# First expert layer: one float32 product split into three fp32r products of leading and trailing bits

## The reference

```python
aff = feats @ centroids.T                 # feats: the layer-normed tokens, 3200 x 256
eid = jnp.argmax(aff, axis=1)             # one expert for each token
xhat = (feats - mu) * jax.lax.rsqrt(var + EPS)
for e in range(E):                        # E = 8, w1[e]: 256 x 1024, w2[e]: 1024 x 256
    mask = (eid == e).astype(feats.dtype)[:, None]
    h = xhat * gamma[e] + beta[e]
    y = feats + jax.nn.relu(h @ w1[e] + b1[e]) @ w2[e] + b2[e]
    alpha = jax.nn.sigmoid(feats @ centroids[e])[:, None]
    out = out + mask * (alpha * y + (1.0 - alpha) * feats)
```

## Time and profile before

| | |
|---|---|
| median of 3 runs | 1718.27 us (1717.52 to 1718.36) |
| the profiled execution | 1719.54 us |
| its span in the profile | 1717.6 us |
| stage `experts` in it: first matmul of tile 0 | 1421.48 us from the start |
| stage `experts` in it: last scatter starts | 1711.74 us from the start |
| mean granted TensorE clock | 0.946 |

### The profile page before, as it was taken

The page is one execution under the profiler, slowest core; times in us unless marked ns, Lnnn a source line. Parts: engine busy times, 40 slices in busy tenths (PEclk is TensorE's granted clock), DMA queues, the critical chain, the costliest instruction groups (busy, mean ns, idle before and its releaser), DMA issues. The chain is left out here.

```text
span 1717.6 us, 39303 instructions
## 1 busy us (share of the span) xinstructions
PE 1512.1 (88%) x12244; PEld 1299.5 (76%) x12244; DVE 1057.3 (62%) x2627; ACT 763.3 (44%) x1830; POOL 426.4 (25%) x564
## 2 busy tenths in 40 slices
PE   4799999999999999829999999999996309999997
PEld 3687878787878787727888888888885307888886
DVE  5658585858585857426777777677773305555553
ACT  3536363646464646314555555655652002222221
POOL 4112121212121211142222222222212153333332
PEclk9999999999999999868999999999997558999999
DMA  5703030303030303057667667677651243555551
GB/s 181 194 1 78 1 76 0 76 0 76 0 76 0 76 0 77 1 131 202 179 184 199 184 183 197 181 192 191 180 135 51 53 134 116 180 184 178 180 179 50
DMA packets 159949, 195.71 MB, mean 114 GB/s; under 512 B 83724, under 2 KB 128307, under 8 KB 159636
## 3 DMA queue, kind: packets, MB, share of 16 engines
q1 hardware_dynamic: 154356, 186.09, 39.7%
q0 software_dynamic: 3968, 6.59, 1.2%
q10 hardware_dynamic: 1568, 2.30, 0.4%
HBM read 138.63 MB, written 58.05 MB: 115 GB/s over the span
## 5 line engine op out<-in xcount | busy, mean ns | idle before, releaser
L1198 DVE TENSOR_REDUCE row_max<-psb_s 100x1 f32<-100x361 f32 x512 | 263.5, 531 | 143.5 <-PE psb_s L1341 137.5
L1090 ACT ACTIVATE probs<-psb_t 121x400 f32<-121x400 f32 (+1 forms) x384 | 190.4, 507 | 114.2 <-PE psb_t L1351 111.7
L419 POOL TENSOR_TENSOR diag<-neg_ident,row_max 100x400 fp32r<-100x400 f32 x128 | 112.2, 898 | 375.1 <-PE ps_t L666 203.6
L1341 PE MATMUL psb_s<-k,q 97*100 97x362 f32 x512 | 186.2, 367 | 15.4 <-DVE row_max L1198 8.3
L1351 PE MATMUL psb_t<-q,k 98*121 98x200 f32 (+1 forms) x768 | 147.4, 274 | 2.6 <-ACT probs L1090 2.0
L2021 PE MATMUL psd_h<-h_in,w_sb 128*128 128x256 f32 x640 | 143.8, 383 | 1.4 <-ACT h_in L1887 1.4
L2029 PE MATMUL psd_y<-w_sb,hid 128*128 128x256 f32 x640 | 144.5, 379 | 0.0
L2021 PEld LDWEIGHTS psd_h<-h_in,w_sb 128*128 128x128 f32 x640 | 123.2, 193 | 19.0 <-issue 1.8
L2029 PEld LDWEIGHTS psd_y<-w_sb,hid 128*128 128x128 f32 x640 | 120.1, 190 | 15.5
L1351 PEld LDWEIGHTS psb_t<-q,k 98*121 98x121 f32 (+1 forms) x768 | 125.5, 184 | 7.6 <-ACT probs L1090 5.1
L376 ACT CAST o_hi<-ps_ot 64x200 fp32r<-64x200 f32 x256 | 82.1, 321 | 100.1 <-PE ps_ot L691 95.2
(11 more groups left out here) (225 smaller groups left out, 3674.7 us busy)
## 6 DMA issues: line engine op xcount, KB each, us to landing
w_sb<-in_w SPq DMA_DIRECT2D x40, 1024.0 KB, 7.8
packed_keys<-k_st SPq DMA_DIRECT2D x32, 724.0 KB, 3.7
k<-packed_keys SPq DMA_DIRECT2D x64, 362.0 KB
v_rows<-v_tok SPq DMA_DIRECT2D x32, 400.0 KB
v_ext<-v_rows SPq DMA_DIRECT2D x32, 400.0 KB
q<-packed_queries SPq DMA_DIRECT2D x64, 200.0 KB
k<-packed_keys SPq DMA_DIRECT2D x64, 181.0 KB
c_t<-in_contextT SPq DMA_DIRECT2D x32, 361.0 KB, 4.6
```

The costliest lines, as they stand in the source:

```text
L419: pool.tensor_tensor(diag[:, g % 2], c.neg_ident[0:S, 0:S].unsqueeze(1).to_broadcast([S, GH, S]), row_max[:, g // 2 % 2, g % 2].unsqueeze( ...
L1090: act.activation(probs[0:KT[kt], u % 2, kt], ps_t[i % 2][0:KT[kt], 0:4 * S], ACT.Exp, scale=HD2 ** -0.5).then_inc(probs_ready, 1)
L1198: dve.reduce_max(row_max[:, p, h:h + 1], ps_s[h % 2][0:S, 0:S2], AX_X).then_inc(max_ready, 1)
L1341: pe.matmul(ps_s[h % 2][0:S, 0:S2E], q2[0:97, p, u, g, S * a:S * (a + 1)], k2[0:97, p, u, g], start=True, stop=True).then_inc(scores_ready, 1)
```

## The change

Each tile's `h_in` and each tile's first-layer weights are split into leading bits (a cast to fp32r) and trailing bits (the difference), and the first layer becomes `split3`. `w1_hi` is made by ACT in two parts of 512 columns, `w1_lo` by POOL in four parts of 256 columns, `h_hi` by ACT and `h_lo` by DVE. The splits of w1 run ahead: at step j ACT makes `w1_hi` of tile j+2, POOL the second half of `w1_lo` of tile j+1 and the first half of that of tile j+2. The load of w1 gets a semaphore of its own and is issued one tile earlier than that of w2. PE waits for `h_lo`, and for `w1_lo` part by part. Some semaphores are made once for all stages.

```diff
@@ experts, SP
                     reach(sp, y_filled, NH * (j - 1))
-                    load_weights(sp, c, e, p, w1, w2)
+                    load_w2(sp, c, e, p, w2)
                 if not last:
                     load_rows(j + 1, 1 - p)
+                    if not (isinstance(j, int) and j < 1):
+                        e = expert_of(sp, c, j + 1)
+                        sp.wait_ge(w1_lo_ready, LO_PARTS * j)
+                        load_w1(sp, c, e, 1 - p, w1)
@@ experts, POOL
+            def trailing_bits(j, p, first, end):
+                for n in range(first, end):
+                    cols = slice(F // LO_PARTS * n, F // LO_PARTS * (n + 1))
+                    pool.wait_ge(w1_hi_ready, j * HI_PARTS + (n * HI_PARTS // LO_PARTS + 1))
+                    pool.sem_inc(pool_passed, 1)
+                    pool.tensor_tensor(w1_lo[:, p, :, cols], c.w1_sb[:, p, :, cols], w1_hi[:, p, :, cols].bitcast(F32),
+                                       ALU.subtract).then_inc(w1_lo_ready, 1)
             prepare(0, 0)
+            trailing_bits(0, 0, 0, LO_PARTS)
+            trailing_bits(1, 1, 0, LO_PARTS // 2)
             def step(j, p, last):
                 if not last:
                     prepare(j + 1, 1 - p)
+                    trailing_bits(j + 1, 1 - p, LO_PARTS // 2, LO_PARTS)
+                if not (isinstance(j, int) and j + 2 >= TILES):
+                    trailing_bits(j + 2, p, 0, LO_PARTS // 2)
                 finish(j, p)
@@ experts, ACT, prepare
                 ins.then_inc(h_in_ready, 1)
+                act.wait_ge(h_in_ready, j + 1)
+                act.sem_inc(act_passed, 1)
+                act.copy(h_hi[:, p], h_in[:, p]).then_inc(h_hi_ready, 1)
                 act.wait_ge(z_ready, j + 1)
                 act.activation(ez[:], z[:], ACT.Exp, scale=-1.0).then_inc(ez_ready, 1)
+            def leading_bits(j, p):
+                act.wait_ge(c.w1_loaded[p], (j - p) * 8 + 16)
+                reach(act, hid_filled, NF * (j - 1))
+                act.sem_inc(act_passed, 1)
+                for n in range(HI_PARTS):
+                    cols = slice(F // HI_PARTS * n, F // HI_PARTS * (n + 1))
+                    act.copy(w1_hi[:, p, :, cols], c.w1_sb[:, p, :, cols]).then_inc(w1_hi_ready, 1)
@@ experts, ACT, step
                 if not last:
                     prepare(j + 1, 1 - p)
+                if not (isinstance(j, int) and j + 2 >= TILES):
+                    leading_bits(j + 2, p)
@@ experts, DVE (behind weigh, ahead of y)
+            def low_inputs(j, p):
+                dve.wait_ge(h_hi_ready, j + 1)
+                dve.sem_inc(dve_passed, 1)
+                dve.tensor_tensor(h_lo[:, p], h_in[:, p], h_hi[:, p].bitcast(F32), ALU.subtract).then_inc(h_lo_ready, 1)
@@ experts, PE
-                pe.wait_ge(c.w_loaded[p], (j - p) * 16 + 32)
-                pe.wait_ge(h_in_ready, j + 1)
+                pe.wait_ge(h_lo_ready, j + 1)
                 for f in range(NF):
                     if f >= 4:
                         copied(j, f - 4)
+                    if f % (NF // LO_PARTS) == 0:
+                        pe.wait_ge(w1_lo_ready, j * LO_PARTS + (f * LO_PARTS // NF + 1))
                     for k in range(KD):
-                        ins = pe.matmul(ps_h[f % 4][:, 0:T], c.w1_sb[:, p, k, 128 * f:128 * (f + 1)], h_in[:, p, k],
-                                        start=(k == 0), stop=(k == KD - 1))
+                        cols = slice(128 * f, 128 * (f + 1))
+                        ins = split3(pe, ps_h[f % 4][:, 0:T], w1_hi[:, p, k, cols], w1_lo[:, p, k, cols],
+                                     h_hi[:, p, k], h_lo[:, p, k], k == 0, k == KD - 1)
                     ins.then_inc(hid_filled, 1)
                 reach(pe, y_ready, NH * j)
+                pe.wait_ge(c.w2_loaded[p], (j - p) * 8 + 16)
```

More of the change, by code:

```diff
@@ L162, in self_attention @@
         ps_y = [ps_p[0], ps_ot]
-        dve_passed = sem("dve_passed_a")
-        pool_passed = sem("pool_passed_a")
+        dve_passed = c.dve_passed
+        pool_passed = c.pool_passed
         x_first = sem("x_first")
@@ L776, in cross_attention @@
         ps_f = psum("psb_f", [128, 512])
-        act_passed = sem("act_passed")
-        dve_passed = sem("dve_passed")
-        pool_passed = sem("pool_passed")
+        act_passed = c.act_passed
+        dve_passed = c.dve_passed
+        pool_passed = c.pool_passed
         w_loaded = sem("w2_loaded")
@@ L1502, in expert_buffers @@
     c.tables = ctx.enter_context(nc.semaphore("tables4"))
-    c.w_loaded = [ctx.enter_context(nc.semaphore(f"w4_loaded{p}")) for p in range(2)]
+    c.w1_loaded = [ctx.enter_context(nc.semaphore(f"w41_loaded{p}")) for p in range(2)]
+    c.w2_loaded = [ctx.enter_context(nc.semaphore(f"w42_loaded{p}")) for p in range(2)]
 def expert_of(eng, c, j):
@@ L1508, in expert_of, with load_w1, load_w2 @@
                           else c.tile_expert[0:1, bass.ds(j, 1)], min_val=0, max_val=E - 1)
-def load_weights(sp, c, e, p, w1, w2):
+def load_w1(sp, c, e, p, w1):
     sp.dma_start(c.w1_sb[:, p], w1[bass.ds(e, 1)].rearrange("o (k p) n -> p (o k) n", p=128)
-                 ).then_inc(c.w_loaded[p], 16)
+                 ).then_inc(c.w1_loaded[p], 16)
+def load_w2(sp, c, e, p, w2):
     sp.dma_start(c.w2_sb[:, p], w2[bass.ds(e, 1)].rearrange("o (k p) n -> p (o k) n", p=128)
-                 ).then_inc(c.w_loaded[p], 16)
+                 ).then_inc(c.w2_loaded[p], 16)
 def route(nc, c, centT, xs, w1, w2, gamma, beta, b1, b2, centroids):
@@ L1594, in _ @@
             for j in range(2):
-                load_weights(sp, c, expert_of(sp, c, j), j, w1, w2)
+                e = expert_of(sp, c, j)
+                load_w1(sp, c, e, j, w1)
+                load_w2(sp, c, e, j, w2)
         @block.gpsimd
@@ L1759, in sem @@
             return ctx.enter_context(nc.semaphore(name))
+        HI_PARTS, LO_PARTS = 2, 4
         NH = T // 128
@@ L1776, in experts @@
         h_in = sb("h_in", [128, 2, KD, T])
+        h_hi = sb("h_hi", [128, 2, KD, T], F32R)
+        h_lo = sb("h_lo", [128, 2, KD, T], F32R)
+        w1_hi = sb("w1_hi", [128, 2, KD, F], F32R)
+        w1_lo = sb("w1_lo", [128, 2, KD, F], F32R)
         hid = sb("hid", [128, NF, T])
@@ L1783, in experts @@
         ps_y = [psum(f"psd_y{i}", [128, 512]) for i in range(NH)]
-        act_passed = sem("act_passed4")
-        dve_passed = sem("dve_passed4")
-        pool_passed = sem("pool_passed4")
+        act_passed = c.act_passed
+        dve_passed = c.dve_passed
+        pool_passed = c.pool_passed
         rows_loaded = [sem(f"rows4_loaded{p}") for p in range(2)]
@@ L1802, in experts @@
         h_in_ready = sem("h_in_ready")
+        h_hi_ready = sem("h_hi_ready")
+        h_lo_ready = sem("h_lo_ready")
+        w1_hi_ready = sem("w1_hi_ready")
+        w1_lo_ready = sem("w1_lo_ready")
         hid_filled = sem("hid_filled")
@@ L1808, in experts @@
         res_ready = sem("res_ready")
-        scattered = [sem(f"scattered{p}") for p in range(2)]
+        scattered = c.scattered
         def over_tiles(eng, emit):
@@ L1889, in prepare @@
                 ins.then_inc(h_in_ready, 1)
+                act.wait_ge(h_in_ready, j + 1)
+                act.sem_inc(act_passed, 1)
+                act.copy(h_hi[:, p], h_in[:, p]).then_inc(h_hi_ready, 1)
                 act.wait_ge(z_ready, j + 1)
                 act.activation(ez[:], z[:], ACT.Exp, scale=-1.0).then_inc(ez_ready, 1)
+            def leading_bits(j, p):
[5 more added lines that the diff above has]
+                    act.copy(w1_hi[:, p, :, cols], c.w1_sb[:, p, :, cols]).then_inc(w1_hi_ready, 1)
+            leading_bits(0, 0)
             prepare(0, 0)
+            leading_bits(1, 1)
             def step(j, p, last):
@@ L1963, in _ @@
             weigh(0, 0)
+            low_inputs(0, 0)
             def step(j, p, last):
@@ L1978, in step @@
                     weigh(j + 1, 1 - p)
+                    low_inputs(j + 1, 1 - p)
                 e = expert_of(dve, c, j)
@@ L2058, in build @@
         c.xs_cleared = ctx.enter_context(nc.semaphore("xs_cleared"))
+        c.act_passed = ctx.enter_context(nc.semaphore("act_passed"))
+        c.dve_passed = ctx.enter_context(nc.semaphore("dve_passed"))
+        c.pool_passed = ctx.enter_context(nc.semaphore("pool_passed"))
+        c.scattered = [ctx.enter_context(nc.semaphore(f"scattered{p}")) for p in range(2)]
         constants(nc, c)
```

## The result

The changed kernel takes 1772.85 us (median of 4 runs, 1771.12 to 1774.69), the kernel before 1718.32 beside it (1717.52 to 1718.98). The ratio is 1.0318, 95% interval 1.0300 to 1.0336: 54.5 us slower, where 4.3 us faster was predicted, and far above the range. The profiled execution has a span of 1769.9 us. Two executions of later versions took 2335 and 2528 us at mean granted clocks of 0.55 and 0.80; they are left out of all medians and ranges.

What follows compares the result with a forecast made beforehand. A turn-to-turn loop through POOL was to bound the kernel at 14.03 us a tile, against 14.25 set by PE. 0.8 - 18 x 0.22 - 1.15 = -4.3 us gave 1714 us, range 1702 to 1724.

Steps and rivals of the forecast that it cites:

- `feats` to the end of `xhat` is 4.01: DVE's stretch ahead of PE's transposes, taken as 4.01 us from the profile of the kernel before.
- the loop's two subtractions: POOL's first half of `w1_lo` of tile j+2, ahead of tile j's scatters: 2.33 us with the step between.
- the scatter's pause: POOL's gap between the subtractions and the first scatter: 0.30 us taken, 0 to 0.88 as bounds.
- The loop: Chain from turn (PE's transposes) to turn through ACT, POOL's subtractions, scatters and inverse root, and DVE's features: 14.03 us.
- the prediction's 14.03: The forecast period of a tile in us, set by the turn-to-turn chain through POOL, against 14.25 before.
- T+3.85: T is the start of PE's transposes; POOL's first-half subtractions were to start 3.85 us later, behind ACT's first `w1_hi` copy.
- PE's price: A tile's first layer as 48 fp32r matmuls 0.12 us apart: 5.76 us instead of 6.91, 1.15 less.
- The `h_lo` wait: PE's wait from the turn to the first layer: T+3.85 against 3.90 before; booked zero, bounds 0 to 0.2 us.
- ACT's splits: ACT's copies: 0.62 us for `h_hi` and 1.04 for each of two `w1_hi` parts; the `w1_hi` copies booked at zero.
- a weight load: w1 was to land about 10.6 us after the first layer's start, ACT wanting it at 12.8; booked zero.
- The first tile's first layer: In tile 0 nothing hides the splitting of `h_in`, so its first layer was to start 1.85 us later than 1421.48.
- The one that ended slower, with the scatters' long pause: Rival: POOL's scatters pause 0.88 us after the subtractions, making the loop 14.61 us and the time 1724; chance 0.20.

Runs made afterwards that it cites:

- e1_gate: The changed kernel, with POOL also waiting for `xhat` of the next tile before the second half of the `w1_lo` subtractions; 1728.12 us, ratio 1.0057 to the kernel before.
- e8_subtract_before_load: The changed kernel with all `w1_lo` subtractions on DVE, two at the top of its step ahead of reading the expert number; 1706.42 us, ratio 0.9935.
- e3_dve_subtracts: The changed kernel with all four `w1_lo` subtractions of a tile on DVE, none on POOL; 1713.08 us, ratio 0.9976 to the kernel before.

## Why the prediction was wrong

**The step that failed** is "`feats` to the end of `xhat` is 4.01". It took the length of a stretch of DVE work from a trace in which POOL did nothing beside `xhat`, and put it into a kernel in which POOL's other two subtractions start the moment `rstd` is out, as `xhat` does. The prediction priced the subtractions as POOL time, and asked what is queued behind them on POOL; it never asked what DVE does beside them. The subtractions of the second half stood in no term of the sum. They cost 2.66 - 0.73 = 1.93 us a tile on the path, 36.7 us in 19 tiles. Two smaller terms were mis-sized: the loop's two subtractions (2.55 to 2.75 us for 2.33) and the scatter's pause, which was 1.17 us for 0.30 in the longer half of the tiles.

**The loop, term by term.** It exists, and with the lock in it every tile adds up. Most tiles of the changed kernel are of two kinds, with periods of 16.2 and 17.4 to 17.5 us. The timeline above shows a long one; two rows of a short one:

```profile
1525.73 2.75 POOL L1892 TENSOR_TENSOR w_lo<-w_sb,w_hi 128x512 fp32r<-128x512 f32 x2 [4.04 <-ACT w_hi L1936]
...
1528.65 1.07 POOL L1881 DMA_INDIRECT out<-res,token  x1 [0.17 <-issue]
```

The terms:

- from the prediction's 14.03; `xhat` +1.93 in both kinds
- the loop's two subtractions were booked at 2.33. In the short tiles they take 2.75, beside `h_lo`, `y` and `res` (+0.42), in the long ones 2.55 (+0.22)
- the scatter's pause was booked at 0.30. It is 0.17 in the short tiles (-0.13) and 1.17 in the long ones (+0.87). It depends on `res`: in the long tiles the scatter starts 0.89 us behind the end of the first `res`, in the short ones 0.17 behind POOL's last subtraction, by when the first `res` has been done for 1.33 us. `res`, whose two tensors both lie in SBUF, is slow beside the subtractions, so its end comes late
- in the long tiles the turn runs at the lower clock, and POOL starts at T+4.30 instead of T+3.85 (+0.45). PE's idle time ahead of the turn doesn't tell the two kinds apart: 2.83 us here, 2.86 in the short tile
- sums: 14.03 + 1.93 + 0.42 - 0.13 = 16.25 (measured 16.23) and 14.03 + 1.93 + 0.22 + 0.87 + 0.45 = 17.50 (measured 17.47).

This working comes from the rows of two tiles. That it is `xhat` which costs most was tested: e1_gate frees it and gives back 44.7 us, the lower clock's share among them. The part of `res` and the scatter alone wasn't tested by itself, but e1_gate has the same two kinds of tile, 14.34 and 15.16 us, with scatter pauses of 0.17 and 1.17. Its short tile is 0.31 over the predicted 14.03: two subtractions of 2.77 instead of 2.33 and a pause of 0.18 instead of 0.30.

**What held.** PE's price, nearly: from the start of a first layer to that of the second it is 6.91 us before and 5.85 in e1_gate and e8_subtract_before_load, 1.06 us less where 1.15 was booked. The `h_lo` wait: in e8_subtract_before_load the first layer starts 3.91 us behind the turn (1546.13 and 1542.22), where 3.85 to 3.90 was worked out; in e1_gate it is 4.15, with `token` and `ez` (0.41 us for 0.17) held beside POOL's subtractions. ACT's splits (0.62 for `h_hi`, 1.98 for both parts of `w1_hi`) and POOL's start: in e1_gate, with a turn at full clock at 1536.02, the first half starts at 1539.86, T+3.84 where T+3.85 was predicted. No engine waits for a weight load in the steady stretch. The first tile's first layer starts at 1423.05, 1.57 us later than before, for 1.85 predicted.

**What the rivals got right.** The one that ended slower, with the scatters' long pause, named a real term: 1.17 us in the long tiles. It is the smaller part. The Trainium skill's GPSIMD Engine Reference, section Engine selection, was quoted against giving POOL this work only for its speed; with the speed of DVE the loop was to be 13.11. e3_dve_subtracts did just that and reached 14.16 (1422.4 to 1691.5): the work then holds POOL's `var_eps` by some 0.3 us, once in one tile and twice in the next. Whether that is all of the 1.05 us between the two isn't shown.

## What to carry to other kernels

Before moving work to POOL, lay DVE's timeline beside it and ask, for each POOL operation with two inputs, which DVE instruction runs at that moment and whether it lies on the critical path: that one can grow by nearly a whole POOL operation, however short it is itself (0.97 us for `xhat`, 0.37 for `token`). `y`, which reads PSUM, did not grow (0.42 us). The slack of an engine is no licence; where the operation lies decides, and one wait that moves it (e1_gate) was worth 44.7 us. That gave back most of the loss and no more: the best of the versions with the split is 0.65% faster than the kernel before, and it has no subtraction on POOL. In a profile the sign is a group whose mean duration grows while its shape stays the same, beside the other engine's work: compare the means of unchanged groups first.

## What the runs showed of the hardware

- POOL with two inputs of 128x512 (1.27 us) against DVE's `tensor_scalar` of 128x256: 0.41 us alone, 1.38 beside it; with pieces of 256 elements a lane 0.81. Each DVE instruction is held by one POOL instruction and ends 0.15 us behind it.
- DVE's `y`, an addition of the same size that reads PSUM, took 0.42 us beside the same POOL operation, as alone.
- It goes both ways: POOL's `var_eps` on 128x2 took 0.50 to 0.59 us instead of 0.22 to 0.27 beside a subtraction on DVE.
- It takes small ones too: in e1_gate `token`, a copy of 128x2, took 0.53 us instead of 0.16.
- A POOL operation with one input of 128x512, though longer (1.52 us), cost `xhat` only 0.40 for two instructions, and `prod`, with two inputs, nothing. It started 0.05 us behind `xhat`, the two-input one 0.06 ahead.
- Reading a register ahead of DVE's work left DVE idle for 0.62 us; issued behind an instruction of 1.3 us it was hidden.
- After 2.83 us without a matmul PE's next four transposes took 1.12 us, at a granted clock of 0.50; after 2.86 us in the tile before they took 0.66, at 1.00.
